# A decoder layer on one core: the feed-forward's preparation spread otherwise over the last two groups of attention, the last probabilities summed by TensorE, and the tokens' weights loaded one tile earlier

## The reference

```python
x = layernorm(tgt, n1)                      # 1: self-attention, causal; a router keeps or masks blocks of 64
q, k, v = split(x @ qkv_w.T)
keep0 = sigmoid(relu(block_mean(k) @ r_w1.T + r_b1) @ r_w2.T + r_b2)[0] > 0.5
p = softmax(where(causal & allowed, q k^T / sqrt(512), ...));  tgt = tgt + (p v) @ sa_out_w.T + sa_out_b
x = layernorm(tgt, n2)                      # 2: cross-attention to ctx_1024, all 1024 keys, no mask
p = softmax(q k^T / sqrt(32));              tgt = tgt + (p v) @ ca_out_w.T + ca_out_b
x = layernorm(tgt, n3)                      # 3: feed-forward, 2048 hidden channels
out = tgt + relu(x @ ff_w1.T + ff_b1) @ ff_w2.T + ff_b2
```

## Time and profile before

| | us |
|---|---|
| median of 3 runs | 3193.87 |
| lowest, highest | 3188.46, 3200.21 |
| the profiled execution | 3189.28 |
| its span, first to last instruction | 3187.6 |
| TensorE busy | 2980.7 (94%) |
| GpSimd busy | 1907.5 (60%) |
| VectorE busy | 1758.3 (55%) |
| ScalarE busy | 1243.5 (39%) |

### The profile page before, as it was taken

One profiled execution on the slowest core, in us unless ns is written; L12 is line 12 of the kernel. 1 busy time (PEld: TensorE's weight loads), 2 busy tenths in 40 slices (PEclk: granted clock), 3 DMA queues, 4 the chain that ended last, 5 costly groups with the idle time before them and its releaser, 6 DMA issues.

```text
span 3187.6 us, 39475 instructions
## 1 busy us (share of the span) xinstructions
PE 2980.7 (94%) x15242; PEld 1966.3 (62%) x15242; DVE 1758.3 (55%) x2864; ACT 1243.5 (39%) x2335; POOL 1907.5 (60%) x991
## 2 busy tenths in 40 slices
PE   7999999999999959789999999999879999999999
PEld 6888886444444427664444444444348888888887
DVE  4455656777777535666777777777742222222221
ACT  2212222555555533325666666666532111111111
POOL 3324333888888775437888888888768343333432
PEclk8999999999999979999999999999989999999999
DMA  6555774445455135734234242332122101011000
GB/s 208 176 165 186 227 220 127 107 108 111 108 117 116 41 119 184 212 133 105 63 72 89 54 104 57 79 82 58 54 67 89 40 27 40 14 40 33 34 14 14
DMA packets 199538, 310.17 MB, mean 97 GB/s; under 512 B 15011, under 2 KB 93363, under 8 KB 199347
## 3 DMA queue, kind: packets, MB, share of 16 engines
q1 hardware_dynamic: 199350, 307.64, 35.3%
HBM read 189.04 MB, written 117.44 MB: 96 GB/s over the span
## 4 chain that ended last, share of the span: by engine, by line
PE 53%; DVE 5%; DMA 2%; POOL 1%; issue 1%; ACT 1%; SPq 1%; DVEq 0%; POOLq 0%; ACTq 0%
PE m_ring L89 13%; PE m_o_ps L89 10%; PE e_st L1217 8%; PE e_pv L1229 7%; PE e_nat L1200 7%; PE c_ring L89 5%; PE e_st L1241 2%; DVE e_neg_max L1110 2%; DMA e_qs<-e_max_lo 1%; DMA c_x<-in_x 1%; DVE m_xt_lo L1577 1%; DMA c_w_raw<-in_ca_in_w 0%; DVE m_xt_hi L1575 0%; DVE m_ow_lo L1595 0%; DVE m_xn L1570 0%
## 5 line engine op out<-in xcount | busy, mean ns | idle before, releaser
L1054 POOL TENSOR_TENSOR e_probs<-e_probs 128x2048 f32<-128x2048 f32 x160 | 732.7, 4585 | 146.5 <-ACT e_probs L1029 141.7
L1029 ACT ACTIVATE e_probs<-e_st 128x512 f32<-128x512 f32 x1024 | 558.1, 598 | 361.5 <-PE e_st L1217 344.0
L1110 DVE TENSOR_REDUCE e_neg_max<-e_nat 128x1 f32<-128x1024 f32 x512 | 603.0, 1217 | 141.6 <-PE e_nat L1200 136.7
L1029 ACT ACTIVATE b_probs<-b_st 128x512 f32<-128x512 f32 (+3 forms) x768 | 340.4, 491 | 278.6 <-PE b_st L1217 269.5
L1107 DVE CUSTOM_DVE_ANT_0 b_nat<-b_nat,mask_qk 128x128 f32<-128x128 f32 (+7 forms) x512 | 374.4, 784 | 80.8 <-PE b_nat L1200 79.6
L1217 PE MATMUL e_st<-e_qs,e_ks 98*128 98x512 f32 x1024 | 396.3, 431 | 22.6 <-DVE e_turned_sums L1128 12.3
L1545 POOL TENSOR_TENSOR m_hid_lo<-m_hid,m_hid_hi 128x512 fp32r<-128x512 f32 x128 | 168.3, 1315 | 386.5 <-DVE m_hid_hi L1583 386.5
L1054 POOL TENSOR_TENSOR b_probs<-b_probs 128x1536 f32<-128x1536 f32 (+3 forms) x128 | 374.7, 2927 | 38.0 <-PE b_pv L1229 35.1
L1583 DVE CAST m_hid_hi<-m_hid 128x512 fp32r<-128x512 f32 x128 | 60.4, 472 | 575.4 <-ACT m_hid L1459 575.4
L1200 PE MATMUL e_nat<-e_ks,e_qs 96*128 96x512 f32 x1024 | 327.5, 401 | 26.2 <-DVE e_neg_max L1110 26.2
L1217 PEld LDWEIGHTS e_st<-e_qs,e_ks 98*128 98x128 f32 x1024 | 176.2, 189 | 275.9 <-ACT e_probs L1029 188.7
(11 more groups left out here) (182 smaller groups left out, 5164.0 us busy)
## 6 DMA issues: line engine op xcount, KB each, us to landing
b_qs<-sq_hi SPq DMA_DIRECT2D x32, 512.0 KB, 6.7
b_ks<-sk_hi SPq DMA_DIRECT2D x32, 512.0 KB, 11.1
e_qs<-cq_hi SPq DMA_DIRECT2D x32, 512.0 KB, 6.8
e_ks<-ck_hi SPq DMA_DIRECT2D x32, 512.0 KB, 13.4
ck_hi<-p_part_hi SPq DMA_DIRECT2D x32, 256.0 KB, 3.3
ck_lo<-p_part_lo SPq DMA_DIRECT2D x32, 256.0 KB, 3.7
cv<-p_tok_out SPq DMA_DIRECT2D x32, 256.0 KB, 3.0
p_x<-in_x SPq DMA_DIRECT2D x8, 1024.0 KB, 7.4
```

What stands on the lines that cost most here:

```text
L1029: act.activation(probs[:, home(n, k), j, first:TOK], st_ps[:, bank_at("scores", blk), first:TOK], ACT.Exp).then_inc(exped, 1)
L1054: pool.tensor_tensor(into, into, probs[:, home(n, k), :, first:TOK], ALU.add).then_inc(added, 1)
L1110: dve.tensor_reduce(neg_max[:, u:u + 1], found, AX.XY, ALU.max, negate=True).then_inc(maxed, 1)
```

## The change

Five things, each visible in the diff. The tokens' weight pieces 8 to 11 are loaded during tile 0 and then two per tile, so that each is loaded one tile before it is split. In the last group of either attention, the steps in `direct` (the last LATE + 1 that are rests: steps 10 and 11 in self-attention, 15 in cross-attention) are not added by GpSimd; TensorE takes them into its sum by ones directly. The lead on VectorE: `ow` and `o` go to steps 14 and 15 of group 14, `bias` to step 4 of group 15, the joins and mixes one step later (5 to 8), `aggregate` to step 8 behind the last join, `norm` to step 11. The first four feed-forward pieces (AHEAD is 2 instead of 3) are loaded before the store of group 15's first half, rounded by ScalarE at steps 14 and 15, and their rests are made by VectorE at step 15 instead of by GpSimd afterwards. In the feed-forward's first tile, splits run two chunks ahead instead of three.

```diff
@@ Projections.sync
-                if q < 2 and i < 6:
-                    load_piece(self.AHEAD + 2 * i + q)
+                if i == 0 and q < 4:
+                    load_piece(self.AHEAD + q)
+                elif q < 2 and 1 <= i < 5:
+                    load_piece(self.AHEAD + 2 * i + 2 + q)
@@ attention
+    direct = [k for k in range(NS - LATE - 1, NS) if k in rests]
+    def added_by_pool(n, k):
+        return k in rests and not (n == N - 1 and k in direct)
@@ attention.sync, main
-                store(n, 0)
-                beside(n, NS)
+                beside(n, 1)
+                store(n, 0)
@@ attention.gpsimd, main
-                    if n * NS + k >= LATE and (k - LATE) % NS in rests:
+                    if n * NS + k >= LATE and added_by_pool(*divmod(n * NS + k - LATE, NS)):
@@ attention.tensor, sum_up
-            for k in firsts_of[h]:
+            tiles = firsts_of[h] + [k for k in rests if steps[k][0] == h and not added_by_pool(n, k)]
+            for k in tiles:
+                first = steps[k][2] if k in rests else 0
                 for j in range(HG):
-                    last = pe.matmul(st_ps[j * DH:(j + 1) * DH, bank, :], ones[:], probs[:, home(n, k), j, :], ...
+                    last = pe.matmul(st_ps[j * DH:(j + 1) * DH, bank, first:TOK], ones[:],
+                                     probs[:, home(n, k), j, first:TOK], ...
@@ tail
-    AHEAD = 3
+    AHEAD = 2
@@ tail.scalar: main no longer splits the first pieces, lead does
+            elif what == "weights":
+                split_w(arg)
@@ tail.gpsimd: the lead "weights" and the first splits of main are gone
@@ tail.vector, lead
+            elif what == "weights":
+                for u in range(2 * AHEAD):
+                    dve.wait_ge(w_hi_done, u + 1)
+                    dve.tensor_tensor(pieces[u][2], pieces[u][3], pieces[u][1].bitcast(F32),
+                                      ALU.subtract).then_inc(first_lo_done, 1)
@@ last_stages, SyncE: m_lead("weights") at (N - 1, 1), before the store, instead of (N - 1, 2 * KT)
@@ last_stages, ScalarE
+                    elif n == N - 1 and k >= 2 * KT - 2:
+                        m_lead("weights", 2 * (k - 2 * KT + 2))
+                        m_lead("weights", 2 * (k - 2 * KT + 2) + 1)
@@ last_stages, VectorE
+                    if n == N - 2 and k == 2 * KT - 2:  m_lead("ow")
+                    elif n == N - 2 and k == 2 * KT - 1:  m_lead("o")
+                    elif n == N - 1 and k == 4:  m_lead("bias")
+                    elif n == N - 1 and 5 <= k < 9:  m_lead("join", k - 5), behind the last one m_lead("aggregate")
+                    elif n == N - 1 and k == 11:  m_lead("norm")
                     elif n == N - 1 and k in (12, 13):  m_lead("turn", ...) as before
+                    elif n == N - 1 and k == 2 * KT - 1:  m_lead("weights")
@@ last_stages, TensorE
-                    if n == N - 1 and 4 <= k < 8:
-                        m_lead("mix", k - 4)
+                    if n == N - 1 and 5 <= k < 9:
+                        m_lead("mix", k - 5)
```

More of the change, by code:

```diff
@@ L1234, in sum_up @@
         def sum_up(n, h):
-            rests_of = sum(steps[k][0] <= h for k in rests)
+            rests_of = sum(steps[k][0] <= h and added_by_pool(n, k) for k in rests)
             pe.wait_ge(added, n * len(rests) + rests_of)
@@ L1238, in sum_up @@
             bank = bank_at("sums", n * HALVES + h)
-            for k in firsts_of[h]:
+            tiles = firsts_of[h] + [k for k in rests if steps[k][0] == h and not added_by_pool(n, k)]
+            for k in tiles:
+                first = steps[k][2] if k in rests else 0
                 for j in range(HG):
-                    last = pe.matmul(st_ps[j * DH:(j + 1) * DH, bank, :], ones[:], probs[:, home(n, k), j, :],
-                                     start=(k == firsts_of[h][0]), stop=(k == firsts_of[h][-1]),
-                                     skip_group_check=True)
+                    last = pe.matmul(st_ps[j * DH:(j + 1) * DH, bank, first:TOK], ones[:],
+                                     probs[:, home(n, k), j, first:TOK], start=(k == tiles[0]),
+                                     stop=(k == tiles[-1]), skip_group_check=True)
             last.then_inc(summed, 1)
@@ L1469, in main @@
         def main():
-            for u in range(2 * AHEAD):
-                split_w(u)
             act.wait_ge(small_loaded, 16 * 5)
@@ L1518, in lead @@
                 raise_var(0)
-            elif what == "weights":
-                for u in range(4):
-                    split_w(u)
         def main():
-            for u in range(4, 2 * AHEAD):
-                split_w(u)
             for i in range(TILES):
@@ L1649, in bank_free, with weights_ready @@
                 pe.wait_ge({"hidden": relu_done, "mix": joined, "turn": turned_out}[user], count + 1)
+        def weights_ready(u):
+            if u < 2 * AHEAD:
+                pe.wait_ge(first_lo_done, u + 1)
+            else:
+                pe.wait_ge(w_lo_done, u - 2 * AHEAD + 1)
         def mix(i, u):
@@ L1937, in beside_e @@
                 def beside_e(n, k):
-                    if n != N - 1:
-                        return
-                    if k == 0:
+                    if n == N - 2 and k == 2 * KT - 2:
                         m_lead("ow")
-                    elif k == 1:
+                    elif n == N - 2 and k == 2 * KT - 1:
                         m_lead("o")
-                    elif k == 2:
+                    elif n == N - 1 and k == 4:
                         m_lead("bias")
-                    elif 4 <= k < 8:
-                        m_lead("join", k - 4)
-                    elif k == 8:
-                        m_lead("aggregate")
-                    elif k == 10:
+                    elif n == N - 1 and 5 <= k < 9:
+                        m_lead("join", k - 5)
+                        if k == 8:
+                            m_lead("aggregate")
+                    elif n == N - 1 and k == 11:
                         m_lead("norm")
-                    elif k in (12, 13):
+                    elif n == N - 1 and k in (12, 13):
                         m_lead("turn", 2 * (k - 12))
                         m_lead("turn", 2 * (k - 12) + 1)
+                    elif n == N - 1 and k == 2 * KT - 1:
+                        m_lead("weights")
                 c.vector(dve, leading(e_lead))
```

13 lines of the change are left out of this document (6 added, 7 removed).

## The result

| | us (median) | runs | lowest to highest |
|---|---|---|---|
| before | 3193.63 | 4 | 3188.46 to 3200.21 |
| changed | 3167.43 | 4 | 3164.31 to 3169.75 |

The ratio is 0.9917, with a 95% interval of 0.9904 to 0.9930: 26 us faster (22 to 31). Measured again, the changed kernel took 3170.31 us beside 3191.03 of the kernel before (ratio 0.9937, 0.9924 to 0.9949). The forecast was 3169. The profiled execution took 3164.31 us (span 3162.6) against 3189.28: 25.0 us less.

What follows compares the result with a forecast made beforehand. TensorE, busy 94% of the span, was taken as the bound, so only its idle or low-clock time counted. 3189.28 less 19.9 + 1.5 + 1.2 = 22.6 gave 3166.7; the median was put at 3169, range 3157 to 3183 us.

Steps and rivals of the forecast that it cites:

- Part 1: Projections: loading tokens' weights one tile earlier removes three TensorE stops and two low-clock stretches; gain 19.9 us, bounds 3.7 to 20.
- Part 2: End of self-attention: TensorE sums the last probabilities, starting 3.0 us earlier, for 1.5 us of added matmuls; gain 1.5 us.
- Part 3: The seam (last two cross-attention groups to feed-forward start): old stops go, new ones come; gain 1.2 us, bounds -7 to +12.
- (a): Cross-attention groups 14 to 15: moved subtractions delay e_outs' copy, new 7.6 us stall; the 9.20 us wait goes; gain 1.7.
- (b): Last cross-attention group, mixes and joins one step later: 3.09 us wait and its low clock go; 1.6 us wait stays.
- (c): Last cross-attention group, step 12: one m_xn ends per GpSimd instruction; TensorE's turn comes at 2359.7 after a new 12 us stall.
- (d): End of the last cross-attention group: the 3.59 us wait before the sum goes; the store leaves 1.2 us earlier.
- (e): Store to first feed-forward multiply: still 13.7 us, covered by m_o's transfer; the shorter AHEAD brings nothing by itself.
- Rival 1: Last cross-attention group: two m_xn end in each GpSimd gap, the turn comes 6 us earlier; 3162 us, chance 0.12.
- Rival 2: Cross-attention groups 14 to 15: the eight subtractions meet all four GpSimd additions, costing 8 us; 3177 us, chance 0.15.
- Rival 3: Projections, tile 1: the transfers of 42 to 65 us hold up something else; 3186 us, chance 0.08.
- Rival 4: Feed-forward's first tile: with one chunk less ahead, GpSimd's splits hold up each of 14 chunks; 3208 us, chance 0.03.

Runs made afterwards that it cites:

- self_sum_alone: Kernel before with only self-attention's last two steps summed by TensorE: 3188.87 us, 0.9987 of before.
- o_split_later: Changed kernel with ScalarE's splits of m_o one chunk later in the feed-forward (SPLIT_AT of 1): 3162.98 us, 0.9913 of before.
- all_three: Changed kernel with the edits of norm_unblocked, copy_unblocked and o_split_later together: 3146.74 us, 0.9846 of before.
- after_again: Changed kernel, unchanged, measured again beside its variants: 3170.31 us, 0.9937 of before.
- weights_alone: Kernel before with only the tokens' weights loaded one tile earlier: 3173.23 us, 0.9940 of before.
- seam_alone: Changed kernel with the tokens' weight loads and self-attention's sum put back as before: 3195.30 us, 1.0007 of before.
- norm_unblocked: Changed kernel with tiles 10, 12, 13 and 15 of cross-attention's last group all summed by TensorE, not GpSimd: 3158.15 us, 0.9899 of before.
- copy_unblocked: Changed kernel with tiles 13 and 15 of cross-attention's last group but one summed by TensorE, not GpSimd: 3161.88 us, 0.9916 of before.

## Why the prediction was right

**Part 1, 19.9 us predicted, 20.3 in the trace, 19 (15 to 23) by its own kernel.** By the starts of the transposes in the two traces each term can be read: 12.3 for the 12.11; 2.2 for the first low clock (2.4); 2.5 for the 2.29; 1.65 for the second low clock (1.7); 1.6 for the 1.40. The terms hold because every transfer that was late had a whole tile in hand afterwards, and the waits after show no new one. The DMA share stayed at 1.05, so it was the order of issue and not the amount that made the pieces late. The issues came at 28.1 and 30.9, not at 26 and 29; nothing hung on that.

**Part 2, 1.5 us predicted.** The step "it can now start when the last weighing ends" held: the sum starts right behind it. The price of the 16 matmuls was the mis-sized term. The trace gave 3.4 us for the end of self-attention, self_sum_alone 2.6, since the sum of 40 ran partly at the higher clock (0.66 and 0.57 granted, where the 24 ran at 0.51). The sum also starts 0.40 us behind the start of the last weighing and not 0.65. The durations of the earlier trace rows are nearly all at the low level; taken as the cost of eight matmuls they are too high as soon as the level changes. Why it rose earlier in one kernel than in the other was not separated.

**Part 3, 1.2 us predicted, 0.5 in the trace, -2 (-5 to +1) by its own kernel.** The near zero was right, and for the reason given: two stops go, two come.
(a) The weighing was to stop for 7.6 us; it stopped for 7.46, behind the eight subtractions, of which only the first two met an addition each. GpSimd fell idle as said. What was wrong is the step "both restart at the lower clock, but now four to five microseconds of it lie before the sum": it lasted from 2274.25 to 2284, nearly 10 us, as these windows show (length, busy, granted clock, DMA share, GB/s):

```profile
2274.00:2276.00 2.00, 1.75 (x8) 0.50 0.00 0
...
2282.00:2284.00 2.00, 2.00 (x9) 0.51 0.00 0
2284.00:2286.00 2.00, 2.00 (x24) 1.00 0.00 0
```

So step 2 followed step 1 by 4.1 us and not by 2.6, and the weighing of step 4 gained -0.7 us against before (2314.22 less 2290.96, less the 23.97 of the stretch) and not +1.7.
(b) The 3.09 us went (0.18 left), and the 1.57 stayed. (c) Each m_xn ended with one instruction of GpSimd: 14.93 us for four, and a stop at the turn of 11.07, predicted 12. With the 23.97 added the turn came at 2361.6, where 2359.7 was predicted: most of the 2.4 us lost in (a). (d) The 3.59 us went, and from the turn to the end of the sum it took 13.4 us where 14.6 were predicted (low clock until about 2342 only). The store came 0.5 us earlier, not 1.2. (e) From the store 13.63 us to the first multiply, predicted 13.7: AHEAD brought nothing there, because ScalarE still waited for m_o. The prediction's list of stops left out the 3.00 us before the first matmul of the feed-forward, and its (e) did not see the 2.75 us that the shorter AHEAD puts before the third chunk. Neither moves the first multiply, which m_o's transfer sets in both kernels; the second is what o_split_later and all_three are left with.
The sum had two errors on how long the low clock lasts, -2.4 and +1.2; the rest came close to what was worked out.

**What fitted by luck.** The forecast put the median 2.3 us above the sum. The median lay 3.1 us above the profiled execution at first and level with it in after_again, so this step was a guess that came out. The three parts make 24.2 in the trace against 22.6. The rest of the 25.0, +0.7, is the start (-1.4, the first transfers), the time behind the first multiply (+0.5), and differences of -3.3, +1.4 and +3.4 in between. All three go with moments of low clock that come in one execution and not in the other. For the -3.3 they are in the last section. For the +1.4 they stand before the end of self-attention: 0.57, 0.50 and 0.65 in the 12 us from 1104 in the kernel before, 0.66 and 0.50 in the 8 us from 1088 in the changed one. The +3.4 is won in mixing, by 1427.77 of the kernel before (1403.93 after: 23.84), and not in cross-attention. Between 1329 and 1405 the shift grows from 19.3 to 23.8 in three steps of 1.5 us, and in the same stretch the clock of the kernel before falls three times (for example 0.57 from 1364 to 1368, where the changed one has 1.00). Nothing shows that these belong to the change: weights_alone, self_sum_alone and seam_alone together leave 5 us or less for it (0.9934 against 0.9937 and 0.9917).
The 0.5 us of part 3 is luck as well. From e_max_lo to the first multiply, the same code took 108.4 us in the trace of before and 111.0 in that of weights_alone; the seam of the change took 107.8, 107.2 and 110.8 in the traces of the changed kernel, after_again and seam_alone. One trace of each can't show a gain of 0.5 or 1.2 us; that it is near zero is shown by the 12 runs of seam_alone.

**The rivals.** Rival 1 (two m_xn per gap of GpSimd) did not happen: 14.93 us is one for each of four instructions. Rival 2 (the eight subtractions meet all four additions) did not happen either: the m_o_lo took 2.48, alone. Rival 3 fell with weights_alone. Rival 4 (GpSimd's splits hold up the feed-forward) fell: the feed-forward's shift changes by +0.5 us.
On the rule of the Trainium skill (SBUF — State Buffer, "Who interferes with whom"): the second transpose of the inversion, at 2322.03, ran while GpSimd added without a gap, and took 0.71 us, as it did at 2329.27 in norm_unblocked with GpSimd idle. By the rule an instruction with at most one SBUF input, outside the two-port modes, does not contend, and here it did not. The same section counts a tensor_tensor with both inputs in SBUF, and a tensor_scalar in a two-port mode, among those that do. m_ow_lo is the first and was held up (10.8 for 2.5 us). m_xn is a tensor_scalar and was held up too (14.9 for 2.85); that it ran in a two-port mode no row says, only that the shortest m_xn of the changed kernel took 0.54 us where an m_ow_lo alone takes some 0.62. That two instructions would pass between additions was the prediction's own conclusion from the section's words on issue order, which do not say how many pass. The traces show one VectorE instruction for each of GpSimd's.

**What the seam is limited by.** norm_unblocked and copy_unblocked show the cause and not only the coincidence: the same instructions at the same place in the queue took 2.85 and 2.48 us once GpSimd's additions were given to TensorE, and the two stops of 11.07 and 7.46 us went with them. Moving VectorE's work to another step, as the change does, moved the stop; taking the other engine's work away removed it.

## What to carry to other kernels

Where a transfer is late behind full queues, look at when it was issued and not how much is moved: one tile earlier was worth 19 of the 21 to 26 us here. Where a long queue of VectorE work is slow only beside GpSimd, moving it along the time axis exchanges one stop for another; see first whether the neighbour's work can be taken elsewhere. Even TensorE, the busiest engine, was the right place here: 8 matmuls, 0.9 us together, for each addition of 4.6. Count an idle stretch of TensorE with the low clock behind it, and give that a range rather than a value.

## What the runs showed of the hardware that was not expected

- How long TensorE stayed at the lower level after a stop does not follow the stop's length. After 9.20 us idle the clock was up again some 4 us on, after 7.46 us idle some 10, after 11.07 some 4.5. After 3.09 us idle it was low for over 9. At the third chunk's first matmul it fell after 2.75 us idle in the changed kernel (0.50 from 2360 to 2362), and after 2.7 in all_three it did not fall at all (window below: 1.00 over the restart). What sets this was not separated.

```profile
2347.00:2352.00 5.00, 3.02 (x12) 1.00 1.05 371
```

- The clock can drop in one execution and not in another, at the same work and behind the same short pauses. The changed kernel had 0.57 and 0.62 at two places in the first 540 us, the first of them behind pauses of 0.93 and 0.24 us,

```profile
471.00:475.00 4.00, 4.00 (x11) 0.57 0.26 97
```

and the kernel before 1.00 at the same work, behind the same two pauses:

```profile
490.00:494.00 4.00, 4.00 (x19) 1.00 0.24 88
```

self_sum_alone, whose code is that of the kernel before up to the end of self-attention, had 0.57 in this very window, 490 to 494. So the drop does not belong to an edit. Each costs 1.5 to 1.7 us. A few of them more or less are the size of the self-attention sum's whole gain, so single traces can't be compared closer than that without a look at the clock.
